# Where the membrane recursion of a spiking delta-rule layer is stepped: eight groups in the front stage, spikes as bytes

## The chip, the cores and the metric

The kernel runs on one core of a Trainium2 chip. The metric is the device time of one execution in microseconds (us), as a median over runs. The engines are TensorE (PE; its weight loads, PEld, overlap the matmuls), VectorE (DVE), ScalarE (ACT), GpSimd (POOL) and SyncE (SP), whose queue issues most transfers. Each engine works through its own list of instructions in order; the lists meet at semaphores. L12 means line 12 of the kernel before.

## The reference, cut to what matters

A two-layer decoder over 64 sequences of 64 positions and 128 features. The change touches one part of layer 1, the delta-rule attention with a spiking neuron: 8 heads of 64 units, so 512 units, each with its own potential `mem` that is stepped along the 64 positions.

```python
q, k, v = heads(h @ Wq), heads(h @ Wk), heads(h @ Wv)   # h: rms norm, causal conv, silu
drive = heads(h @ Wspike, dk)
alpha_base = heads(silu(h @ Wau + bau) @ Wad + bad, dk)
beta_base = h @ Wbeta + bbeta

def step(carry, ins):
    s, mem = carry
    qt, kt, vt, dt, at, bt = ins
    mem = DECAY * mem + dt                      # 0.9
    spike = (mem > THR)                         # 0.5, the forward value
    mem = mem - spike * THR
    alpha = sigmoid(at + asp * spike)           # decay of the state, per unit
    beta = sigmoid(bt + sum(spike * bsp))       # step size, per head
    active = sum(abs(spike)) > 0
    alpha = where(active, alpha, 1); beta = beta * active
    s = s * alpha; pred = kt @ s
    s = s + (beta * kt) (vt - pred)
    return (s, mem), qt @ s
```

The potential depends on `drive` and on nothing of the delta rule, and the delta rule needs the spikes alone.

## The kernel before

The whole decoder is one program of stages one after the other (`run_stage`), each closed by a barrier of all engines. The 4096 tokens stand in NG = 8 groups of T = 512 tokens, that is GB = 8 sequences of S = 64 positions. Features or units lie on the partitions; the 512 units make HDP = 4 blocks of 128, so the drives of one group are 128 partitions x 4 x 512 fp32 values, with position t of every sequence 64 values (256 bytes) apart. Two stages matter.

**Front stage** (`delta_front`, tag "front"). Per group: GpSimd normalises the tokens twice (`zr` for the convolution, L1848, and `zt` for the gate, L1855; group 0's `zr` is VectorE's, L1989); TensorE turns both (L1870, L1876), makes the gate (L1883, L1890) and the drives (L1899, four banks); ScalarE empties the banks (L1959 writes the drives, doubled, so that the threshold is 1); VectorE runs the 4-tap convolution (`conv`, L2006 and L2008). Groups 0 and 1 keep their drives in SBUF, groups 2 to 7 share two buffers and are sent to DRAM (`drive_rows`, L1822 and L1824), 1 MB each. VectorE steps the potential of groups 0 and 1 together: one step is `m = drive[t] - 0.9 * mem` in place (L1997) and `mem = (m > 1) - m` (L1999), both on 128x64 values, each waiting for the one before through a semaphore (`link`). Twenty-four steps are laid between the convolutions of groups 4 to 7, forty behind them. Then two comparisons of 128x2048 make spikes of the potentials (L2023 for group 1, sent to `drive_rows`; L2024 for group 0, put where the next stage reads it).

**Delta stage** (`delta`, tag "delta"). A software pipeline of iterations -2 to 8. In iteration `it` the core is group `it` (chunked delta rule: TensorE's products L2272 and L2285, inverse L2309 and L2331, values and outputs), `front` prepares group `it + 1` (keys, queries, decays, norms), `tail` finishes group `it - 1` (norm, output product, feed-forward), and the order on each engine is written out by hand. The spikes of a group lie in `SPK[g % 2]`. VectorE steps the potential of group `it + 2` (`membrane`, L2820 to L2828, 128x32 values, 127 instructions a group, groups 2 to 7, so iterations 0 to 5) in pieces of 26, 14, 10, 7 and 7 positions between its other work; the first piece stands between `turned(it, 2)` and `masked(it, 5)`, a masked copy (L2778) that TensorE's next products wait for. GpSimd's last work of an iteration is `z_tok` (L2711) and `spikes` (L2687), the comparison of 128x2048 in place. Readers of the spikes are TensorE (`f_cb`, L2205) and VectorE (`f_al`, L2880). SP's queue loads `h`, drives and gates, in one order (`load_h`, `load_drive`, `load_gate`).

## Time and profile before

| | us |
|---|---|
| median of 3 runs | 2706.17 (2694.99 to 2707.96) |
| span of the profiled execution | 2686.7 |
| busy PE / PEld | 2239.4 (83%) / 1568.4 (58%) |
| busy DVE / ACT / POOL | 1613.9 (60%) / 982.9 (37%) / 782.4 (29%) |
| front stage, about | 954 to 1048 |
| delta stage, about | 1049 to 2220 |

The profiled execution's own time is its span of 2686.7 us; the median of the runs lies 19.5 us above it. Busy shares are means over stages with different limits. In a timeline row the first number is the start, the second the time from there to the end of the last of the merged instructions, and brackets give the idle time ahead of it with who ended it. Matmuls are pipelined with modelled ends, so a busy PE need not be PE at its peak.

### The profile page before, as it was taken

How to read it: one execution, taken by the hardware profiler on the slowest of the kernel's cores; microseconds unless marked ns; L12 is line 12 of the kernel's file. 1: busy time of each engine (PE TensorE's matmuls, PEld its weight loads, DVE VectorE, ACT ScalarE, POOL GpSimd, SP SyncE). 2: the span in 40 equal slices, each digit the busy share in tenths (PEclk: the TensorE clock that was granted, in tenths of full speed). 3: DMA queues.
4: the chain of work that ended last, by engine and by line, in shares of the span. 5: the costliest groups of instructions: out<-in, count | busy, mean ns of one | idle time of the engine just before them, and what ended most of it. 6: DMA issues, size and time to landing. Idle time of an engine off the chain costs nothing. (4 is left out here: it accounts for less than half of the span.)

```text
span 2686.7 us, 73844 instructions
## 1 busy us (share of the span) xinstructions
PE 2239.4 (83%) x31032; PEld 1568.4 (58%) x31071; DVE 1613.9 (60%) x4219; ACT 982.9 (37%) x1930; POOL 782.4 (29%) x884
## 2 busy tenths in 40 slices
PE   7898989898877865889999999999999986964675
PEld 4566666666665632465666666666666756653453
DVE  4565555555454366677778787868664713467444
ACT  3444443434322343334343434343434331321222
POOL 0111111111104671325152524343342300111774
PEclk9999998989757977789999999999999975555987
DMA  4000000000021223000000000000000002000114
GB/s 162 9 1 9 9 9 1 5 1 1 1 75 33 62 81 126 6 3 26 3 26 3 26 3 22 7 22 7 3 7 3 7 1 97 2 29 12 52 52 123
DMA packets 42504, 75.78 MB, mean 28 GB/s; under 512 B 5988, under 2 KB 27244, under 8 KB 39620
## 3 DMA queue, kind: packets, MB, share of 16 engines
q1 hardware_dynamic: 35140, 56.63, 6.1%
q0 software_dynamic: 7040, 14.43, 1.9%
q8 instruction: 252, 4.13, 0.6%
q14 instruction: 72, 0.59, 0.1%
HBM read 46.73 MB, written 24.31 MB: 26 GB/s over the span
## 5 line engine op out<-in xcount | busy, mean ns | idle before, releaser
L2778 DVE COPY_PREDICATED delta_neg_a_and_p_t<-delta_level_int,bank 128x256 f32<-128x256 uint8 x384 | 179.3, 536 | 62.5 <-PE bank L2285 62.1
L2309 PEld LDWEIGHTS bank<-delta_inverse,delta_neg_a_and_p_t 64*64 64x64 f32 x5120 | 169.5, 140 | 45.8 <-issue 45.8
L2309 PE MATMUL bank<-delta_inverse,delta_neg_a_and_p_t 64*64 64x64 f32 x5120 | 191.8, 227 | 0.0
L2682 POOL TENSOR_TENSOR delta_scaled_beta_k<-delta_scaled_beta_k,delta_decays 128x256 f32<-128x256 f32 x160 | 124.3, 777 | 221.4 <-issue 162.7
L2512 ACT ACTIVATE delta_two_less_ax<-bank 128x512 f32<-128x512 f32 x160 | 94.9, 597 | 240.4 <-PE bank L2309 238.8
L683 POOL TENSOR_TENSOR attn_probs<-attn_probs,attn_row_sum 128x512 f32<-128x512 f32 x64 | 65.4, 1043 | 385.1 <-DVE attn_row_sum L766 385.1
L2285 PE MATMUL bank<-weights_sb,delta_scaled_beta_k 64*64 64x64 f32 x6144 | 128.0, 228 | 47.9 <-DVE delta_neg_a_and_p_t L2778 43.5
L2285 PEld LDWEIGHTS bank<-weights_sb,delta_scaled_beta_k 64*64 64x64 f32 x6144 | 109.6, 140 | 84.1 <-DVE delta_neg_a_and_p_t L2778 51.1
L303 PE MATMUL bank<-attn_z_self_t,weights_sb 128*128 128x256 f32 x512 | 144.5, 431 | 16.9 <-DVE attn_cross_values L741 12.5
L312 PE MATMUL bank<-attn_w_value_out,attn_z_self_t 128*64 128x512 f32 x512 | 142.5, 682 | 2.0 <-DVE attn_z_value_out L706 1.4
L2331 PE MATMUL bank<-delta_two_less_ax,delta_inverse_t 64*64 64x64 f32 x4096 | 139.0, 223 | 4.1 <-issue 3.9
L2331 PEld LDWEIGHTS bank<-delta_two_less_ax,delta_inverse_t 64*64 64x64 f32 x4096 | 132.5, 140 | 5.6 <-issue 5.3
L750 DVE TENSOR_REDUCE attn_row_max<-bank 128x8 f32<-128x512 f32 x128 | 82.4, 686 | 84.0 <-PE bank L392 54.4
L2518 ACT ACTIVATE delta_inverse<-bank 128x512 f32<-128x512 f32 x128 | 76.4, 598 | 148.8 <-PE bank L2331 148.6
L303 PEld LDWEIGHTS bank<-attn_z_self_t,weights_sb 128*128 128x128 f32 x512 | 102.6, 212 | 44.9 <-issue 22.0
L2185 PE MATMUL bank<-delta_head_rows,norm_sel 16*128 16x512 f32 x192 | 114.5, 699 | 7.8 <-DVE delta_head_rows L2892 3.6
L574 ACT ACTIVATE attn_z_value_out<-bank 128x512 f32<-128x512 f32 x96 | 57.1, 595 | 163.2 <-PE bank L312 163.2
L2700 POOL TENSOR_TENSOR delta_kq_squared<-weights_sb 128x512 f32<-128x512 f32 x64 | 70.8, 1137 | 110.6 <-PE bank L2180 103.8
L1411 POOL DMA_INDIRECT moe_z_sorted<-z_rows,moe_take_row x71 | 68.7, 968 | 106.8 <-DVE moe_take_row L1718 85.5
L2803 DVE TENSOR_TENSOR weights_sb<-weights_sb,delta_decays 128x512 f32<-128x512 f32 x128 | 98.2, 767 | 0.0
L691 POOL TENSOR_TENSOR x_all<-x_all,attn_out_bias 128x256 f32<-128x256 f32 x16 | 11.6, 727 | 278.1 <-DVE attn_z_tokens L786 278.1
L2683 POOL TENSOR_TENSOR delta_decays<-delta_decays 128x256 f32<-128x256 f32 (+4 forms) x160 | 91.7, 573 | 0.0
(545 smaller groups left out, 5139.9 us busy)
## 6 DMA issues: line engine op xcount, KB each, us to landing
delta_drives<-front_drive SPq DMA_DIRECT2D x7, 1024.0 KB, 3.9
weights_sb<-in_w_moe_dram SPq DMA_DIRECT2D x1, 4352.0 KB, 14.8
z_rows<-moe_z_all SPq DMA_DIRECT2D x16, 256.0 KB, 2.3
delta_odd_spikes<-delta_drives SPq DMA_DIRECT2D x4, 1024.0 KB, 5.0
weights_sb<-moe_outs SPq DMA_DIRECT2D x8, 512.0 KB, 7.2
weights_sb<-delta_drives SPq DMA_DIRECT2D x3, 1024.0 KB, 5.0
weights_sb<-in_w_delta_dram SPq DMA_DIRECT2D x1, 2816.0 KB, 9.9
weights_sb<-in_ctx_tok_dram SPq DMA_DIRECT2D x8, 264.0 KB, 5.6
```

Of the source, the lines that this page charges most:

```text
L303: last = pe.matmul(out_[:, i * 256:(i + 1) * 256], wA[:, 0 if kind == "q" else 1, m * 128:(m + 1) * 128], zA[:, g % 2, :], start=True, sto ...
L312: last = pe.matmul(out_[64 * hh:64 * hh + 64, :], zA[:, g % 2, 64 * b:64 * b + 64], vo[:, hh, 512 * half:512 * half + 512], start=True, st ...
L750: dve.tensor_reduce(mx[:, o % 2, h, :], ps[h], AX, ALU.max).then_inc(s["max"], 1)
L2185: return pe.matmul(out_[:, :], nsel[r, j, :], hrows[r, :], start=start, stop=True)
L2285: last = pe.matmul(two[eo][rows(sg), b4 * 64:b4 * 64 + 64], kr[r, hp, t], second(kq[r, g % 2, :, hp, t], c), start=b < 2, stop=True, skip_ ...
L2309: last = pe.matmul(out_[rows(sg), u], AP[rows(sg), hp, eo, b4, 0, :], X[rows(sg), hp, u], start=False, stop=True, skip_group_check=True)
L2331: last = pe.matmul(out_[rows(sg), u], lhsT, rhs, start=b == 0, stop=True, skip_group_check=True)
L2512: act.activation(W[:, hp, :], bank[4 + hp % 2][:, :], ACT.Copy).then_inc(s["w"], 1)
L2682: pool.tensor_tensor(r_[:, :, 0, :], r_[:, :, 0, :], a_[:, :, 1, 0:1].to_broadcast([128, T // (2 * c), c]), ALU.mult)
L2683: pool.tensor_tensor(a_[:, :, 0, 0:1], a_[:, :, 0, 0:1], a_[:, :, 1, 0:1], ALU.mult).then_inc(s["scaled_kr"], 1)
L2778: last = dve.copy_predicated(second(AP[:, hp, eo, :, :, :].rearrange("p b i n -> p (b i) n"), c), m_, PAIR[hp % 2][eo][:, :].rearrange("p ...
L2803: dve.tensor_tensor(v, v, f.unsqueeze(1).to_broadcast([128, 2, m, c]), ALU.mult).then_inc(s["scaled_kq"], 1)
```

## The change

The front stage keeps the drives of all eight groups in SBUF (64 KB per partition), sends none to DRAM, and steps the eight potentials together once the last drive is there: the same 64 positions, each instruction now on 128x256 values, still 64 values apart. None of it lies between the convolutions any more. Then the comparison of group 0 goes to its place in fp32, and those of groups 1 to 7 write bytes (128x2048 uint8) into two buffers, sent to DRAM at 256 KB each; from group 3 on VectorE waits until the buffer's last transfer has landed. GpSimd no longer normalises `zr`: VectorE does it for all groups, two ahead of the convolution, into a part of the weights' region.

In the delta stage the potentials' steps are gone from VectorE. SP loads bytes into one buffer (group g + 1 after GpSimd has widened group g), and GpSimd's comparison becomes a copy from uint8 to fp32 at the same place of its list, for group 1 too, in iteration -1; its wait for the last step becomes waits for the transfer and for the last readers of the buffer that it writes. Two small casts whose results nobody reads (`selb`, `lmi`) leave the end of the attention stage.

```diff
@@ attention stage, end
-                    dve.tensor_copy(selb[:, :, :], self_[:, :, :])
-                    dve.tensor_copy(lmi[:, :, :], lm[:, :, :])
@@ delta_front
-                drive = sb("drive", [128, 4, HDP, T], ctx=ctx)
-                mem = sb("membrane", [128, 2 * HDP * GB], ctx=ctx)
+                drive = sb("drive", [128, NG, HDP, T], ctx=ctx)
+                mem = sb("membrane", [128, NG * HDP * GB], ctx=ctx)
+                spk8 = sb("spike_bytes", [128, 2, HDP, T], U8, ctx=ctx)
...
+                    for g in range(1, NG):
+                        sp.wait_ge(s["spikes"], g + 1)
+                        sp.dma_start(spike_rows[g, :, :, :], spk8[:, g % 2, :, :]).then_inc(spikes_out[g % 2], 16)
...
-                                last = pool.tensor_scalar(zr[:, g % 2, i, :], x_all[:, k, :], mv_all[:, k, 0:1], rms[:, k:k + 1],
...
+                    every = drive[:, :, :, :].rearrange("p g j (b t) -> p (g j b) t", t=S)
 
                     def membrane(t):
-                        m_ = two[:, :, t]
+                        m_ = every[:, :, t]
...
+                    z_rms(0)
+                    z_rms(1)
                     dve.wait_ge(s["pads"], 1)
-                    for g in range(4):
+                    for g in range(NG):
+                        if g + 2 < NG:
+                            z_rms(g + 2)
                         conv(g)
-                    dve.wait_ge(s["drive"], 2 * HDP)
...
+                    dve.wait_ge(s["drive"], NG * HDP)
+                    for t in range(S):
                         membrane(t)
-                    dve.tensor_scalar(drive_of(1), drive_of(1), 1.0, None, ALU.is_gt).then_inc(s["spikes"], 1)
                     dve.tensor_scalar(spk0, drive_of(0), 1.0, None, ALU.is_gt).then_inc(s["spikes"], 1)
+                    for g in range(1, NG):
+                        if g >= 3:
+                            dve.wait_ge(spikes_out[g % 2], 16 * ((g - 1) // 2))
+                        dve.tensor_scalar(spk8[:, g % 2, :, :], drive_of(g), 1.0, None, ALU.is_gt).then_inc(s["spikes"], 1)
@@ delta, SP
-                        sp.dma_start(SPK[g % 2][:, :, :], drive_rows[g, :, :, :]).then_inc(s[f"drive_in{g % 2}"], 16)
+                            sp.wait_ge(s["spikes"], g - 1)
+                        sp.dma_start(spk8[:, :, :], spike_rows[g, :, :, :]).then_inc(s["spikes_in"], 16)
@@ delta, GpSimd
                     def spikes(g):
-                        pool.wait_ge(s["potential"], g - 1)
-                        pool.tensor_scalar(SPK[g % 2][:, :, :], SPK[g % 2][:, :, :], 1.0, None, ALU.is_gt).then_inc(s["spikes"], 1)
+                        pool.wait_ge(s["spikes_in"], 16 * g)
+                        if g >= 2:
+                            pool.wait_ge(s["cb_ps"], nth_of("cb", g - 2))
+                            pool.wait_ge(s["al_rd"], nth_of("al", g - 2, 3))
+                        pool.tensor_copy(SPK[g % 2][:, :, :], spk8[:, :, :]).then_inc(s["spikes"], 1)
@@ delta, VectorE
-                        drive = core and it + 2 < NG
-                        if drive:
-                            membrane(it + 2, 0, 26)
...
-                            membrane(it + 2, 57, S)
```

## Rows read from the trace of the kernel before

**Rows 1.** Busy time by window (PE, PEld, DVE, ACT, POOL; clock), iterations 5 and 6.

```profile
1786.60:1926.30 139.70, 131.16 (x2656) 88.06 (x2655) 108.29 (x264) 58.26 (x100) 52.71 (x59) 0.98 0.02 5
1926.30:2061.60 135.30, 130.33 (x2654) 86.60 (x2654) 75.18 (x138) 57.65 (x99) 47.07 (x58) 0.97 0.02 5
```

**Rows 2.** Timeline of PE: one product of iterations 0, 5 and 6.

```profile
1175.61 0.60 PE L2285 MATMUL bank<-weights_sb,delta_scaled_beta_k 64*64 64x64 f32 x12 [5.00 <-DVE delta_neg_a_and_p_t L2778]
...
1868.31 0.51 PE L2285 MATMUL bank<-weights_sb,delta_scaled_beta_k 64*64 64x64 f32 x18 [3.80 <-DVE delta_neg_a_and_p_t L2778]
...
2004.27 0.52 PE L2285 MATMUL bank<-weights_sb,delta_scaled_beta_k 64*64 64x64 f32 x20 [0.60 <-DVE delta_neg_a_and_p_t L2778]
```

**Rows 3.** Timeline of DVE, iteration 0: last step of the first piece, then masked copy.

```profile
1174.53 0.23 DVE L2828 SCALAR_TENSOR_TENSOR delta_membrane<-weights_sb 128x32 f32<-128x32 f32 x1
1174.79 0.43 DVE L2778 COPY_PREDICATED delta_neg_a_and_p_t<-delta_level_int,bank 128x256 f32<-128x256 uint8 x1
```

**Rows 4.** Groups by line on PE, iteration 5: busy us, mean ns.

```profile
L2161 PE MATMUL bank<-group_conv_out,small_sb 128*64 128x512 f32 x2 | 1.1, 618 | 0.0
```

**Rows 5.** By line: duration min/median/max in ns, first and last start, forms.

```profile
L2826 DVE SCALAR_TENSOR_TENSOR weights_sb<-delta_membrane,weights_sb x186: 204/217/1798, 1158.2 to 1779.9; 128x32 f32<-128x32 f32 x186
L2828 DVE SCALAR_TENSOR_TENSOR delta_membrane<-weights_sb x189: 182/229/1034, 1158.0 to 1780.2; 128x32 f32<-128x32 f32 x189
L1997 DVE SCALAR_TENSOR_TENSOR front_drive<-front_membrane,front_drive x63: 267/278/291, 988.5 to 1042.1; 128x64 f32<-128x64 f32 x63
L1999 DVE SCALAR_TENSOR_TENSOR front_membrane<-front_drive x63: 297/301/436, 988.2 to 1041.8; 128x64 f32<-128x64 f32 x63
```

**Rows 6.** Groups by line and shape on DVE: contiguous values, two lengths.

```profile
L2898 DVE SCALAR_TENSOR_TENSOR delta_scaled_beta_k<-weights_sb,bank 128x512 f32<-128x512 f32 x32 | 21.9, 686 | 47.6 <-PE bank L2185 47.4
L3308 DVE SCALAR_TENSOR_TENSOR gated_weights_t<-bank,gated_decay 128x256 f32<-128x256 f32 x32 | 11.6, 415 | 11.7 <-ACT gated_decay L3218 11.7
```

**Rows 7.** Timeline of DVE: steps at the front stage's end, comparison, next stage.

```profile
1024.75 0.28 DVE L1997 SCALAR_TENSOR_TENSOR front_drive<-front_membrane,front_drive 128x64 f32<-128x64 f32 x1
...
1042.14 0.28 DVE L1997 SCALAR_TENSOR_TENSOR front_drive<-front_membrane,front_drive 128x64 f32<-128x64 f32 x1
1042.45 1.23 DVE L2023 TENSOR_SCALAR front_drive<-front_drive 128x2048 f32<-128x2048 f32 x1
...
1048.82 0.41 DVE L2901 TENSOR_SCALAR delta_half_head_norm<-small_sb 128x4 f32<-128x4 f32 x1 [4.00 <-PEq L118]
```

**Rows 8.** Timeline of ACT: the front stage's last drive.

```profile
1022.85 0.60 ACT L1959 ACTIVATE front_drive<-bank 128x512 f32<-128x512 f32 x1 [0.26 <-PE bank L1899]
```

**Rows 9.** Timeline of PE, front stage: a wait for GpSimd.

```profile
967.70 0.69 PE L1876 MATMUL bank<-const_sb,front_z_tok 128*128 128x128 f32 x2 [1.91 <-POOL front_z_tok L1855]
```

**Rows 10.** The transfers: timeline of SP, by tile (`delta_h`, 256 KB), the page (1 MB).

```profile
1043.71 0.32 SPq L1826 DMA_DIRECT2D delta_drives<-front_drive  x1
...
DMA to landing us min/median/max: 2.0/2.5/3.2
...
delta_drives<-front_drive SPq DMA_DIRECT2D x7, 1024.0 KB, 3.9
```

**Rows 11.** Timeline of DVE: end of the attention stage, start of the next.

```profile
776.37 0.67 DVE L910 CAST sel_bf<-sel_f 8x1024 bf16<-8x1024 f32 x1
776.97 0.24 DVE L911 CAST level_int_sb<-level_sb 128x192 uint8<-128x192 f32 x1
778.31 0.29 DVE L1162 BATCH_NORM_STATS2 moe_bn_stats<-x_all 128x6 f32<-128x128 f32 x1 [1.10 <-PEq L118]
```

**Rows 12.** Timeline of POOL, iterations 5 and 6; a plain copy of the size by line.

```profile
1920.69 5.37 POOL L2687 TENSOR_SCALAR delta_odd_spikes<-delta_odd_spikes 128x2048 f32<-128x2048 f32 x1 [11.93 <-DVE delta_odd_spikes L2824]
1931.64 1.27 POOL L2704 TENSOR_TENSOR delta_two_less_ax<-delta_two_less_ax,delta_o_rstd 128x512 f32<-128x512 f32 x1 [5.57 <-ACT delta_o_rstd L2488]
...
L2671 POOL COPY delta_neg_a_and_p_t<-delta_neg_eye x8: 1890/1926/1927, 1075.4 to 2038.8; 128x2048 f32<-128x2048 f32 x8
```

**Rows 13.** Timeline of PE: first matmul of the delta stage.

```profile
1048.82 1.08 PE L2161 MATMUL bank<-group_conv_out,small_sb 128*64 128x512 f32 x1 [26.00 <-PEq L118]
```

More of the change, by code:

```diff
@@ L1806, in drive_of @@
                 def drive_of(g):
-                    return drive[:, g if g < 2 else 2 + g % 2, :, :]
+                    return drive[:, g, :, :]
                 h_out = [s["h_out0"], s["h_out1"]]
                 gate_out = [s["gate_out0"], s["gate_out1"]]
-                drive_out = [s["drive_out0"], s["drive_out1"]]
+                spikes_out = [s["spikes_out0"], s["spikes_out1"]]
                 @block.sync
@@ L1829, in _ @@
                         sp.wait_ge(gate_out[k], 16 * (NG // 2))
-                        sp.wait_ge(drive_out[k], 16 * (NG // 2 - 1))
-                    sp.wait_ge(s["spikes_out"], 16)
+                        sp.wait_ge(spikes_out[k], 16 * len(range(k or 2, NG, 2)))
                 @block.gpsimd
@@ L1842, in _ @@
                     for g in range(NG):
-                        if g >= 1:
-                            if g >= 2:
-                                pool.wait_ge(s["z_rms_ps"], g - 1)
-                            for i in range(4):
-                                k = 4 * g + i
-                                last = pool.tensor_scalar(zr[:, g % 2, i, :], x_all[:, k, :], mv_all[:, k, 0:1], rms[:, k:k + 1],
-                                                          ALU.subtract, ALU.mult)
-                            last.then_inc(s["z_rms"], 1)
                         if g >= 2:
@@ L1987, in _, with z_rms @@
                     dve.wait_ge(s["rstd"], 1)
-                    for i in range(4):
-                        last = dve.tensor_scalar(zr[:, 0, i, :], x_all[:, i, :], mv_all[:, i, 0:1], rms[:, i:i + 1], ALU.subtract, ALU.mult)
-                    last.then_inc(s["z_rms0"], 1)
-                    two = drive[:, 0:2, :, :].rearrange("p g j (b t) -> p (g j b) t", t=S)
+                    def z_rms(g):
+                        if g >= 2:
+                            dve.wait_ge(s["z_rms_ps"], g - 1)
+                        for i in range(4):
+                            k = 4 * g + i
+                            last = dve.tensor_scalar(zr[:, g % 2, i, :], x_all[:, k, :], mv_all[:, k, 0:1], rms[:, k:k + 1],
+                                                     ALU.subtract, ALU.mult)
+                        last.then_inc(s["z_rms"], 1)
+                    every = drive[:, :, :, :].rearrange("p g j (b t) -> p (g j b) t", t=S)
                     def membrane(t):
-                        m_ = two[:, :, t]
+                        m_ = every[:, :, t]
                         if t >= 1:
@@ L2753, in _ @@
                             z_tok(it)
-                            if it + 2 < NG:
-                                spikes(it + 2)
+                        if 1 <= it + 2 < NG:
+                            spikes(it + 2)
                 @block.vector
@@ L2816, in turned @@
                         dve.transpose(XT[:, hp, :], X[:, hp, :]).then_inc(s["x_t"], 1)
-                    def membrane(g, t0, t1):
-                        dve.wait_ge(s[f"drive_in{g % 2}"], 16 * (g // 2 + g % 2))
-                        rows_ = SPK[g % 2].rearrange("p h (b t) -> p (h b) t", t=S)
-                        for t in range(t0, t1):
-                            m_ = rows_[:, :, t]
-                            if t == S - 1:
-                                dve.scalar_tensor_tensor(m_, mem[:, :], -0.9, m_, ALU.mult, ALU.add).then_inc(s["potential"], 1)
-                            elif t >= 1:
-                                link(dve.scalar_tensor_tensor(m_, mem[:, :], -0.9, m_, ALU.mult, ALU.add))
-                            if t < S - 1:
-                                link(dve.scalar_tensor_tensor(mem[:, :], m_, 1.0, m_, ALU.is_gt, ALU.subtract))
                     def t_gated(g):
@@ L2987, in _ @@
                             f_bk(it + 1)
-                        if drive:
-                            membrane(it + 2, 26, 40)
                         if tail:
@@ L3000, in _ @@
                             f_beta(it + 1)
-                        if drive:
-                            membrane(it + 2, 40, 50)
                         if front:
                             f_kr(it + 1, 0)
-                        if drive:
-                            membrane(it + 2, 50, 57)
                         if tail:
                             t_out(it - 1)
-                        if drive:
-                            membrane(it + 2, 57, S)
                         if front:
@@ L3014, in _ @@
                             f_kr(it + 1, 3)
-            run_stage("delta", "h_in0 h_in1 h_in2 drive_in0 drive_in1 potential spikes gate_in const_set masks au_ps au_rd k_ps k_rd q_ps q_rd al_ps al_rd nrm_part "
+            run_stage("delta", "h_in0 h_in1 h_in2 spikes_in spikes gate_in const_set masks au_ps au_rd k_ps k_rd q_ps q_rd al_ps al_rd nrm_part "
                                "nrm_rd norm root log_root q_sum logit sigmoid beta row_w bias_ps bias bk_ps bk_rd cb_ps cb_rd kr_ps kr_rd ss_ps ss_rd wo_ps wo_rd zz_ps zz_rd f1_ps f1_rd "
```

54 lines of the change are left out of this document (16 added, 38 removed).

## The prediction

> **What bounds the kernel now.** Read first the windows of the delta loop, cut where each group's first products start. Iteration 5 has steps of the potential on VectorE, iteration 6 has none, and the rest of their work is alike: a comparison that the kernel itself makes. Iteration 5 takes 139.7 us with VectorE busy for 108.3 us and TensorE for 131.2 us; iteration 6 takes 135.3 us with VectorE at 75.2 us and TensorE at 130.3 us [rows 1]. So the steps are 33.1 us of VectorE's time per iteration, and 4.4 us of the loop's. TensorE sets the pace; VectorE matters only where TensorE waits for it. Read next TensorE's timeline for its waits. There is one large one per iteration, at the products behind `masked(it, 5)`: 5.00 us in iteration 0, 3.80 us in iteration 5, 0.60 us at the same place of iteration 6 [rows 2]. VectorE's timeline says why: the masked copy follows the last step of the 26-position piece without a gap [rows 3]. The other pieces stand where TensorE has enough to do. Of the 4.4 us, 3.2 us is this wait; 1.1 us is a pair of matmuls (`f_au`) that iteration 6 no longer has [rows 4].
>
> The front stage ends otherwise. Its last drive is written at 1023.45 us [rows 8]; from then VectorE alone steps on until 1042.4 us, then come one comparison, its transfer and the barrier, and the delta stage starts at 1048.8 us [rows 7]. What is put there has no cover at all.
>
> **Delta loop: what goes.** Six iterations lose their steps. The excess of the wait over iteration 6's 0.60 us goes: 4.4 us in iteration 0, and in iterations 1 to 5 3.2 us each (they show the same wait, 3.8 us): 4.4 + 5 x 3.2 = 20.4 us. What is late next is TensorE's own list, as in iteration 6. Bounds: 16 us, if part comes back as other waits; 27 us, 6 x 4.5, if all of the difference between the two windows were due to the steps.
>
> GpSimd's comparison took 5.37 us and stood behind a wait of 11.93 us for the last step [rows 12]. In its place comes a copy from bytes. No row has that form; the nearest are a plain fp32 copy of the size, 1.93 us, and the comparison itself, 5.37 us [rows 12]. It can start when `z_tok` is done, 11.93 us earlier than now, and the next work of GpSimd needs ScalarE's result at 1931.6 us, about 23 us after `z_tok`'s end [rows 12]. So even 5.37 us are covered by TensorE's values and outputs: 0 us. If that cover were gone, 6 x 5.4 = 32 us. GpSimd's new waits are for readers of the iteration before, long done. SP's load of the bytes of group `g + 3` now waits for that copy, and the gate of group `g + 1` is queued behind it; the gate is read an iteration later, so nobody waits. A load of 256 KB for 1 MB costs nothing more.
>
> **Front stage up to the last drive.** VectorE gets 28 more normalisations of 128x128, four a group, and loses the 24 steps (six a group) that stood between the last four convolutions; it is idle for most of each group there, which passes at TensorE's pace, so they cost nothing; a group's four hold a quarter of the values of one comparison of 1.23 us [rows 7], so with their fixed parts about 1.2 us a group, 8 us in all if that cover were gone. GpSimd keeps half of its work; TensorE's early waits for it, such as 1.91 us [rows 9], shrink. I take 2 us off (0 to 4), so the last drive is there at 1021.4 us, not 1023.45 us. The longer idle time of TensorE that follows should cost nothing: already after 26.00 us idle its first matmul pass takes 1.08 us against 0.62 us in the loop [rows 4, 13], so it starts at the lower of its two levels in either kernel.
>
> **The steps at 256 values.** This term decides. At 128x64 the undisturbed pace, from the step at 1024.75 us to that at 1042.14 us, 27 pairs on, is 17.39 / 27 = 0.644 us a pair [rows 7]: 0.278 + 0.301 us busy [rows 5] and 0.065 us between. For the length the same two instructions stand in the trace at 32 values: 0.217 and 0.229 us [rows 5]. So 32 more values cost 0.061 + 0.072 = 0.133 us a pair, 1.9 and 2.25 ns a value. From 64 to 256 values are six such steps: 0.644 + 6 x 0.133 = 1.44 us. Reckoned instead as 0.15 us fixed and the rest per value (2.0 and 2.36 ns) it is 1.48 us. I take 1.45 us; 63 pairs are 91.4 us. The lower bound is the price of contiguous values: (686 - 415) / 256 = 1.06 ns each [rows 6]; 0.644 + 2 x 192 x 0.00106 = 1.05 us, so 66.2 us. The strided pairs are themselves measured at two lengths, so I stay at their end; the upper bound is 1.50 us, 94.5 us.
>
> Against 19.0 us of steps behind the last drive now, 91.4 us is +72.4 us.
>
 The trace agrees, with 1.9 to 2.25 ns a value.
>
> **Comparisons and transfers at the end.** Group 0: 1.15 us (the pitch of the two now). Bytes out: a cast of 192 values to bytes took 0.24 us [rows 11], little over the fixed part, so writing bytes keeps the fast rate, and I take 1.15 us for each of seven too. From group 3 on each waits for the transfer of two before it: 256 KB land 2.5 us after their issue [rows 10], say 2.6 us with the semaphores. The comparisons end at 1.15, 2.3, 4.9, 6.05, 8.65, 9.8 and 12.4 us. Then the last landing, 2.6 us, and 1.2 us to the next stage (now: issued at 1043.7, landed 3.9 us later, next stage at 1048.8 [rows 7, 10]). In all 1.15 + 12.4 + 2.6 + 1.2 = 17.4 us against 6.4 us now: +11.0 us. At one value per cycle (2.3 us each) the chain ends at 17.3 us: 5 us more.
>
> **Attention stage.** The two casts end that stage [rows 11]; without them the barrier comes 0.9 us earlier.
>
> **The sum.** -0.9 - 2.0 + 72.4 + 11.0 - 20.4 = +60.1 us. Span 2686.7 + 60.1 = 2746.8 us. The median of the runs lies 19.5 us above the profiled span; 2706.2 + 60.1 = 2766 us. With the terms at their ends it reaches from 2755 us (27 us gained in the loop, 4 us in the front, pair at 1.42 us) to 2780 us (16 us, 0 us, 1.50 us, slow comparisons).
>
> **The rivals.**
> - One cycle a value. The excess at 64 values could be a fixed latency, so that longer instructions pay 1.06 ns a value. For it: the contiguous rows [rows 6]. Against it: the slope between 32 and 64 values, which holds no fixed part [rows 5]. The steps are 66.2 us, 25 us less: 2741 us.
> - VectorE bounds the loop. If iterations were as long as VectorE's list makes them, each of six would lose its 33.1 us: 198.6 us in place of 20.4 us, so 2588 us, faster than before. For it: VectorE is busy for 78% of iteration 5 and has the largest wait of TensorE. Against it: iteration 6, which is free of the steps, is 4.4 us shorter, not 33. It decides from (60.1 + 20.4) / 6 = 13.4 us an iteration upwards; all of TensorE's idle time in iteration 5 is 8.5 us [rows 1].
> - The widening becomes the wait. If the copy from bytes ran against VectorE so that both stood still, up to 5.4 us in each of seven iterations would show: +38 us, 2804 us. For it: GpSimd's copy moves into a stretch where VectorE works. Against it: the cover of 23 us.
> - The steps stay hidden. Should the scheduler of the front let part of them run before the last drive, there would be less; but the wait for all 32 drives stands in front of the first step, so I give this nothing.
>
> **How the numbers follow.** Forecast 0.82; one cycle a value 0.12; VectorE's loop 0.02; widening 0.04. The range takes in the bounds of the forecast, half of the second case, and some 6 us of spread as in the runs shown: 2742 to 2786 us. A measurement of this kernel can tell about 0.5%, 13.5 us, from no change. Faster: 0.02. Within 0.5%: 0.02, if the first rival meets a larger gain in the loop. Slower: 0.96.
>
> **What would show it.** Right: steps of 128x256 at 0.64 to 0.76 us each and a pair every 1.45 us; a front stage that is some 80 us longer, with TensorE idle for over 100 us at its end; iterations 1 to 5 of 136.5 us, the wait at 0.6 us; bytes compared in 1.2 us, with waits of about 1.4 us for landings; GpSimd's copy under 5.4 us. Wrong: steps at 0.42 to 0.50 us, iterations below 130 us, or a copy that TensorE or VectorE waits for.

## The result and the profile after

The changed kernel takes 2769.4 us (median of 4 runs, 2753.6 to 2777.1) against 2702.4 us (median of 4 runs, 2695.0 to 2708.0) of the kernel before, measured beside it: a ratio of 1.0241, 95% interval 1.0204 to 1.0277 (estimated over the runs, so it isn't the quotient of the two medians). Single executions can take hundreds of microseconds longer with no change of the code (one of `e_pieces` took 3250.8 us, the other five 2676.7 to 2689.8 us); ratios and their intervals leave such executions out, medians don't. The change makes the kernel slower by 2.4%. Its profiled execution has a span of 2751.8 us, 65.1 us more than the one of before; forecast were +60.1 us.

The same boundaries read in both traces tell where the 65.1 us lie:

| stretch | before | after | difference | forecast |
|---|---|---|---|---|
| attention stage, to the first instruction of the next | 778.3 | 785.9 | +7.6 | -0.9 |
| first mixture of experts | 176.3 | 176.2 | -0.1 | 0 |
| front stage, from `front_taps` to the delta stage's first instruction | 94.2 | 172.7 | +78.5 | +81.4 |
| delta stage up to the first products | 49.2 | 49.7 | +0.5 | 0 |
| iterations 0 to 5 of the delta loop | 828.3 | 803.3 | -25.0 | -20.4 |
| iteration 6 to the end | 760.4 | 764.0 | +3.6 | 0 |

First the windows of iterations 5 and 6 of the kernel after, to be held against [rows 1]. The columns are window, length, then busy time with instructions of PE, PEld, DVE, ACT and POOL, granted clock, DMA share, GB/s.

```profile
1850.80:1987.80 137.00, 131.47 (x2653) 87.17 (x2652) 75.23 (x138) 58.23 (x100) 48.88 (x59) 0.98 0.02 5
1987.80:2122.80 135.00, 130.16 (x2654) 87.59 (x2653) 75.00 (x138) 57.67 (x99) 47.08 (x58) 0.97 0.02 5
```

VectorE is busy for 33 us less in iteration 5 than it was, and the iteration is 2.7 us shorter. Its own iteration 6 takes 135.0 us, against 135.3 us before.

The wait that the forecast named, in the timeline of PE at the same product of iteration 4 of after (start, duration, instruction, idle time before it in brackets):

```profile
1793.42 0.39 PE L2272 MATMUL bank<-weights_sb,delta_scaled_beta_k 64*64 64x64 f32 x10 [0.60 <-DVE delta_neg_a_and_p_t L2768]
```

It is 0.60 us, which iteration 6 showed in the kernel before [rows 2].

The front stage's end, in the instructions on `front_drive` of after, grouped by line (duration in ns: minimum, median, maximum; first and last start; form):

```profile
L1986 DVE SCALAR_TENSOR_TENSOR front_membrane<-front_drive x63: 724/727/732, 1024.7 to 1117.9; 128x256 f32<-128x256 f32 x63
L1984 DVE SCALAR_TENSOR_TENSOR front_drive<-front_membrane,front_drive x63: 702/705/711, 1025.5 to 1118.6; 128x256 f32<-128x256 f32 x63
```

And the timeline of DVE of after, from the first step through the comparisons to the delta stage, to be held against [rows 7]:

```profile
1024.73 0.73 DVE L1986 SCALAR_TENSOR_TENSOR front_membrane<-front_drive 128x256 f32<-128x256 f32 x1 [11.73 <-ACT front_drive L1940]
...
1119.38 1.23 DVE L2010 TENSOR_SCALAR weights_sb<-front_drive 128x2048 f32<-128x2048 f32 x1
1120.52 2.36 DVE L2014 TENSOR_SCALAR front_spike_bytes<-front_drive 128x2048 uint8<-128x2048 f32 x2
1123.79 2.36 DVE L2014 TENSOR_SCALAR front_spike_bytes<-front_drive 128x2048 uint8<-128x2048 f32 x2 [0.91 <-DMA delta_spikes<-front_spike_bytes]
1127.05 2.38 DVE L2014 TENSOR_SCALAR front_spike_bytes<-front_drive 128x2048 uint8<-128x2048 f32 x2 [0.90 <-DMA delta_spikes<-front_spike_bytes]
1130.33 1.23 DVE L2014 TENSOR_SCALAR front_spike_bytes<-front_drive 128x2048 uint8<-128x2048 f32 x1 [0.90 <-DMA delta_spikes<-front_spike_bytes]
1134.82 0.41 DVE L2877 TENSOR_SCALAR delta_half_head_norm<-small_sb 128x4 f32<-128x4 f32 x1 [3.26 <-PEq L116]
```

VectorE is idle for 11.73 us until the last drive is written at 1024.70 us, then steps for 94.7 us, with TensorE idle all the while, then compares and sends for 15.4 us. The timeline of PE of after gives that idle time at the next stage's first instruction, where [rows 13] had 26.00 us:

```profile
1134.82 1.94 PE L2150 MATMUL bank<-group_conv_out,small_sb 128*64 128x512 f32 x2 [110.75 <-PEq L116]
```

The widening, in the timeline of POOL, iteration 3 of after (compare [rows 12]):

```profile
1696.80 1.89 POOL L2677 CAST delta_odd_spikes<-delta_spike_bytes 128x2048 f32<-128x2048 uint8 x1
1720.06 1.27 POOL L2694 TENSOR_TENSOR delta_two_less_ax<-delta_two_less_ax,delta_o_rstd 128x512 f32<-128x512 f32 x1 [21.37 <-ACT delta_o_rstd L2475]
```

The copy takes 1.89 us and GpSimd is idle for 21.37 us behind it.

### The profile page after: what moved, and what is told of

It reads as the page before. It is cut to its first block and busy times, and to the rows that moved or that the text cites. A ratio compares the mean times of both kernels' runs of the same rounds, so it can differ in the third digit from the quotient of the medians.

```text
span 2751.8 us, 73107 instructions
## 1 busy us (share of the span) xinstructions
PE 2251.6 (82%) x31071; PEld 1573.6 (57%) x31071; DVE 1480.2 (54%) x3495; ACT 982.6 (36%) x1930; POOL 740.3 (27%) x857
## 5 line engine op out<-in xcount | busy, mean ns | idle before, releaser
L2318 PEld LDWEIGHTS bank<-delta_two_less_ax,delta_inverse_t 64*64 64x64 f32 x4096 | 126.7, 135 | 6.5 <-issue 6.2
L748 DVE TENSOR_REDUCE attn_row_max<-bank 128x8 f32<-128x512 f32 x128 | 82.5, 686 | 87.5 <-PE bank L390 57.9
L2843 DVE TENSOR_TENSOR delta_kq_squared<-delta_silu_or_square,bank 128x512 f32<-128x512 f32 x32 | 21.7, 678 | 158.4 <-PE bank L2231 76.4
L2694 POOL TENSOR_TENSOR delta_two_less_ax<-delta_two_less_ax,delta_o_rstd 128x512 f32<-128x512 f32 x32 | 47.5, 1484 | 220.8 <-ACT delta_o_rstd L2475 220.8
L2150 PE MATMUL bank<-group_conv_out,small_sb 128*64 128x512 f32 x16 | 10.3, 733 | 110.8 <-PEq L116 110.8
```

Source lines behind the costliest of these rows:

```text
L748: dve.tensor_reduce(mx[:, o % 2, h, :], ps[h], AX, ALU.max).then_inc(s["max"], 1)
L2318: last = pe.matmul(out_[rows(sg), u], lhsT, rhs, start=b == 0, stop=True, skip_group_check=True)
```

## The experiments

Two chips were used. On the first (`e_pieces`, `e_no_loop_steps`, `e_position_major`, `e_pieces_front`) the kernel before takes 2706.9 us, on the second (the others) 2753.5 us, so times are compared within a chip alone.

**The wait alone (`e_pieces`).** The theory holds that the steps in the loop cost the one wait behind the 26-position piece, not VectorE's 33 us. This kernel is the one before, with the same 64 steps cut at other positions, so that the first piece is shorter.

```diff
-                            membrane(it + 2, 0, 26)
+                            membrane(it + 2, 0, 18)
...
-                            membrane(it + 2, 26, 40)
+                            membrane(it + 2, 18, 32)
...
-                            membrane(it + 2, 40, 50)
+                            membrane(it + 2, 32, 42)
...
-                            membrane(it + 2, 50, 57)
+                            membrane(it + 2, 42, 57)
```

> The kernel before with its steps kept in the delta loop, but cut elsewhere: the first piece has 18 positions in place of 26, the second and third keep 14 and 10, the fourth has 15 in place of 7, the last keeps 7. The number of instructions is the same. Theory: the steps cost the loop only where the first piece makes TensorE wait for masked(it, 5). The piece ends 8 x 0.51 = 4.1 us earlier, so the wait of 3.8 us goes back to 0.6 us (5.0 in iteration 0), iterations 1 to 5 last 136.5 us and not 139.8 us, and the kernel is about 20 us faster than before (ratio 0.9925). The fourth piece has 5.1 us of idle time behind it, so 4.1 us more fit. Rival: it is VectorE's load as a whole that costs, so the wait turns up at another place and the time stays within 5 us of before.

Measured: 2685.9 us, ratio 0.9931 (0.9908 to 0.9953). Iterations 0 to 5 take 125.4, 136.5, 136.4, 136.3, 136.6 and 136.5 us. Its window of iteration 5, columns as above, and the PE row of the product of iteration 0 that waited 5.00 us in [rows 2]:

```profile
1777.70:1914.20 136.50, 130.02 (x2653) 86.72 (x2652) 108.39 (x264) 58.21 (x100) 52.74 (x59) 0.99 0.02 5
```

```profile
1179.97 0.69 PE L2285 MATMUL bank<-weights_sb,delta_scaled_beta_k 64*64 64x64 f32 x32 [0.96 <-DVE delta_neg_a_and_p_t L2778]
```

VectorE is still busy for 108.4 us and the iteration is as short as that of the changed kernel. So all that the change wins in iterations 1 to 5 was to be had by cutting at another position, at no cost elsewhere.

**No steps in the loop (`e_no_loop_steps`).** The kernel before, leaving out the recursion of groups 2 to 7: only one instruction of the last position stays in each, so the spikes of these groups aren't those of the reference.

```diff
-                        for t in range(t0, t1):
+                        for t in range(S - 1 if t1 == S else t1, t1):
...
-                                dve.scalar_tensor_tensor(m_, mem[:, :], -0.9, m_, ALU.mult, ALU.add).then_inc(s["potential"], 1)
+                                dve.tensor_scalar(m_, m_, 1.0, None, ALU.mult).then_inc(s["potential"], 1)
```

> The kernel before without the potentials' steps of groups 2 to 7 in the delta loop (left out: those 127 instructions a group, one of which is replaced by a product with 1; the spikes of these groups are then comparisons of the drives). GpSimd's comparison of 5.37 us stays. Theory: the loop's gain in the changed kernel (25 us in its trace) comes from the steps' going alone: 20 to 26 us less than before, with iteration 0 about 8 us shorter and 1 to 5 about 3.4 us. Rival: part of it comes from GpSimd, whose copy of 1.89 us stands where the comparison of 5.37 us did and can start earlier: then this kernel gains 3.2 us an iteration and only 4.4 us in iteration 0.

Measured: 2689.4 us, ratio 0.9932 (0.9901 to 0.9962). Without any steps it is no faster than `e_pieces` with all of them. Its iterations take 125.4, 138.5, 139.5, 137.2, 139.8 and 137.0 us, 2 us more on average in 1 to 5 than those of `e_pieces`. Here is a part of its iteration 2 in the timeline of PE, and the window around it:

```profile
1444.89 0.69 PE L2285 MATMUL bank<-weights_sb,delta_scaled_beta_k 64*64 64x64 f32 x32 [0.71 <-DVE delta_neg_a_and_p_t L2778]
...
1452.44 4.87 PE L2185 MATMUL bank<-delta_head_rows,norm_sel 16*128 16x512 f32 x6 [0.76 <-DVE delta_kq_squared L2865]
```

```profile
1446.00:1466.00 20.00, 19.08 (x242) 11.50 (x243) 9.04 (x17) 4.02 (x7) 4.31 (x8) 0.74 0.01 2
```

The wait is gone (0.71 us), but at 1452 us six matmuls of the norms take 4.87 us; the same six take 3.02 us in the changed kernel. The granted clock is 0.74 over these 20 us: TensorE falls to its lower level (1.2 GHz) for a part of them. The same happens at 1729 us. What brings such a fall about isn't settled: it came in iterations 2 and 4 and not in 1, 3 and 5, whose instructions are the same.

The expectation was missed: about 18 us came off by the ratio, not 20 to 26, and 3.9 us in iteration 0 (129.3 us before), not 8. That is what its rival said, which gives the rest to GpSimd's shorter copy. The windows of iteration 0 speak against that rival; they are of before, of after, and of this kernel, columns as above:

```profile
1098.00:1227.30 129.30, 114.80 (x2553) 79.00 (x2552) 99.13 (x243) 46.49 (x80) 44.99 (x54) 0.90 0.04 13
1184.50:1305.90 121.40, 111.60 (x2557) 77.57 (x2556) 66.10 (x117) 46.54 (x80) 40.65 (x54) 0.92 0.03 7
1102.10:1227.50 125.40, 116.48 (x2553) 80.72 (x2552) 66.30 (x118) 46.45 (x80) 44.20 (x54) 0.88 0.04 13
```

TensorE is idle for 14.5 us of the iteration before (its length less the busy time), for 9.8 us in the changed kernel and for 8.9 us here, with GpSimd's comparison still in place. So the waits go with VectorE's steps alone. What this kernel lacks there against the changed one is busy time of TensorE, 116.5 us against 111.6 us for the same matmuls, at a granted clock of 0.88 against 0.92.

**The stride (`e_position_major`).** The changed kernel with the drives stored by position, so that the 256 values of a step stand next to each other. ScalarE's writes, the comparisons and the widening take the stride instead.

```diff
-                drive = sb("drive", [128, NG, HDP, T], ctx=ctx)
+                drive = sb("drive", [128, S, NG, HDP * GB], ctx=ctx)
...
-                            act.activation(drive_of(g)[:, j, :], bank[4 + j][:, :], ACT.Copy, scale=2.0).then_inc(s["drive"], 1)
+                            act.activation(drive[:, :, g, j * GB:(j + 1) * GB].rearrange("p t b -> p b t"),
+                                           bank[4 + j][:, :].rearrange("p (b t) -> p b t", t=S), ACT.Copy, scale=2.0).then_inc(s["drive"], 1)
...
-                        m_ = every[:, :, t]
+                        m_ = every[:, t, :]
```

> The changed kernel with the drives laid out by position: the 256 values of one position stand side by side, ScalarE writes them 1 KB apart, the bytes of a group are stored by position and GpSimd's copy puts them back. Theory: the steps of 0.705 and 0.727 us are slow because each value lies 256 bytes from the next; contiguous they take 0.42 us each, a pair 0.91 us with its gaps, 63 pairs 57 us in place of 94.5 us. The comparison for group 0 gets the stride instead (about 4.5 us, 3.3 us more) and ScalarE's writes stay under TensorE's 0.86 us a bank. In all about 34 us less than the changed kernel, so 2735 us, still slower than before. Rival: the time per value is that of the operation, not of the stride: steps stay above 0.65 us and the kernel within 8 us of the changed one.

Measured: 2733.1 us, ratio 1.0113 (1.0087 to 1.0138), so 1.3% less than the change. Its instructions on `front_drive`, by line:

```profile
L1987 DVE SCALAR_TENSOR_TENSOR front_membrane<-front_drive x63: 425/426/427, 1026.8 to 1083.8; 128x256 f32<-128x256 f32 x63
L1985 DVE SCALAR_TENSOR_TENSOR front_drive<-front_membrane,front_drive x63: 425/426/426, 1027.2 to 1084.3; 128x256 f32<-128x256 f32 x63
L1940 ACT ACTIVATE front_drive<-bank x32: 1032/1076/1120, 980.8 to 1025.7; 128x512 f32<-128x512 f32 x32
```

The same operation on the same number of values takes 426 ns in place of 705 and 727 ns: the stride of 64 values (256 bytes) is what costs, not the length. The steps take 57.9 us (1026.8 to 1084.7), 36.8 us less, and the front stage 138.0 us, 34.7 us less. ScalarE's writes go from 597 to 1076 ns, GpSimd's copies, which put the positions back in order, from 1.89 to 3.92 us, and both hide all the same: the last drive is begun 62.9 us into the stage, against 62.0 us, and iterations 0 to 5 take 807.8 us, against 803.3 us, within what executions of the changed loop differ by (803.3 to 810.9 us). The comparison for group 0 takes 1.90 us, not the 4.5 us expected. `VectorE: DVE Perf Modes` (Trainium skill), section The TRN2 errata, gives (N + 151) / 0.96 ns for an fp32 addition of two tensors and names no stride with it. For N = 256 that is an estimate of 424 ns, with which the contiguous steps agree (425 and 426 ns) and the strided ones of the changed kernel don't (705 and 727 ns).

**The fixed part (`e_halves`).** The changed kernel, its 63 pairs of 256 values taken as two runs of 63 pairs of 128.

```diff
-                    for t in range(S):
-                        membrane(t)
+                    for i in range(2):
+                        for t in range(S):
+                            membrane(t, i)
```

> The changed kernel with the front stage's steps on 128x128 values: first all 64 positions of groups 0 to 3, then all of groups 4 to 7, twice as many instructions. Theory: a strided step costs a fixed part and 2.22 ns a value. From 278 and 301 ns at 64 values and 705 and 727 ns at 256 the line gives 420 and 443 ns at 128, a pair every 0.93 us with its gaps, 126 pairs 117 us, 22.5 us more than in the changed kernel. Rival: the cost per value rises with the length (1.9 ns between 32 and 64 values, 2.22 ns between 64 and 256), so at 128 values the steps lie below the line, at 400 and 425 ns.

**The changed kernel again (`e_changed_again`)**, unaltered, on the same chip:

> The changed kernel once more, unaltered. In its trace the first stage, whose code is that of before but for two casts at its end, is 7.6 us longer than in the trace of before, at a granted clock of 0.86 to 0.94 where that had 0.90 to 0.98. Theory: this belongs to the execution, not to the change: the end of the first stage falls somewhere between 778 and 787 us again, while the front stage (172.7 us) and the loop's iterations repeat within 1 us where their clock is the same. Rival: the changed kernel's first stage is always longer, at 785 us or more.

Measured: 2831.5 us for `e_halves`, 2814.8 us for the changed kernel (one run each), 1.022 times the median of before there. The steps of `e_halves`:

```profile
L1989 DVE SCALAR_TENSOR_TENSOR front_membrane<-front_drive x126: 440/443/446, 1042.2 to 1158.5; 128x128 f32<-128x128 f32 x126
L1987 DVE SCALAR_TENSOR_TENSOR front_drive<-front_membrane,front_drive x126: 417/420/424, 1042.6 to 1159.0; 128x128 f32<-128x128 f32 x126
```

With [rows 5] the step of the potential takes 301, 443 and 727 ns at 64, 128 and 256 values, that of the drive 278, 420 and 705 ns: from 64 to 128 and from 128 to 256 the slope is 2.22 ns a value in each, one line. What the line leaves is about 159 and 136 ns of fixed part. The rival, 400 and 425 ns at 128 values, is out. The front stage takes 195.2 us against 172.9 us in the changed kernel again, +22.3 us where the line gave +22.5 us. The two times differ by 16.7 us only, since the attention stage, with the same code, ended at 785.1 us in one and at 791.4 us in the other.

The expectation for the changed kernel again was met by the front stage (172.9 us) and by iterations 3 to 5, within 1.0 us; iterations 0 to 2 took 1.2 to 4.0 us more, at granted clocks of 0.89 and 0.98 against 0.92 and 0.99. The attention stage ended at 791.4 us, outside the 778 to 787 us expected and where the rival had it, at 785 us or more. All four executions traced on this chip ended it there (785.1, 791.4, 793.6 and 794.8 us); none of them is of the kernel before, so this chip can't tell the change from the chip. This execution has a span 61.2 us longer than the first of the same kernel, and most of that lies in stages that the change leaves alone: the first mixture of experts takes 195.0 us, not 176.2 us, and iteration 6 to the end 793.4 us, not 764.0 us.

**The cover of the widening (`e_widen8`).** The changed kernel; GpSimd makes the same copy eight times per group in place of once.

```diff
+                        for n in range(7):
+                            pool.tensor_copy(SPK[g % 2][:, :, :], spk8[:, :, :]).then_inc(s["widened"], 1)
+                            pool.wait_ge(s["widened"], 7 * (g - 1) + n + 1)
                         pool.tensor_copy(SPK[g % 2][:, :, :], spk8[:, :, :]).then_inc(s["spikes"], 1)
```

> The changed kernel with GpSimd's copy from bytes made eight times in place of once for each group, one after the other (15 us more work? no: 8 x 1.89 = 15.1 us in all, 13.2 us more, plus gaps). Theory: GpSimd is idle for 21.4 us behind the copy, so the loop keeps its length: iterations 1 to 5 at 136 to 137 us, and the copy once costs nothing at all. Rival: the copies run against VectorE's work of the iteration's end and delay the next group's start: iterations 2 us longer or more.

Measured: 2816.8 us, 2.0 us over the changed kernel (one run each). In the timeline of POOL:

```profile
1724.15 13.64 POOL L2678 CAST delta_odd_spikes<-delta_spike_bytes 128x2048 f32<-128x2048 uint8 x7
1737.85 1.89 POOL L2680 CAST delta_odd_spikes<-delta_spike_bytes 128x2048 f32<-128x2048 uint8 x1
1747.40 1.27 POOL L2697 TENSOR_TENSOR delta_two_less_ax<-delta_two_less_ax,delta_o_rstd 128x512 f32<-128x512 f32 x1 [7.66 <-ACT delta_o_rstd L2475]
```

13.6 us more of GpSimd per group, beside VectorE's work, leave 7.66 us of its idle time; iterations 0 to 5 take 805.9 us, against 810.9 us in the changed kernel again; the difference lies in iteration 0 (120.2 and 125.3 us), and iterations 1 to 5 take 137.1 us on average in both. Neither a single copy nor eight of them are waited for.

**The front part alone (`e_pieces_front`).** `e_pieces` with what else the change does ahead of the last drive: no two casts, and all normalisations of `z_rms` on VectorE, two groups ahead, none on GpSimd. The steps of groups 0 and 1 stay where they were, five positions a group in place of six.

```diff
-                            for i in range(4):
-                                k = 4 * g + i
-                                last = pool.tensor_scalar(zr[:, g % 2, i, :], x_all[:, k, :], mv_all[:, k, 0:1], rms[:, k:k + 1],
-                                                          ALU.subtract, ALU.mult)
...
+                    z_rms(0)
+                    z_rms(1)
...
-                        for t in range(6 * (g - 4), 6 * (g - 3)):
+                        if g + 2 < NG:
+                            z_rms(g + 2)
+                        for t in range(5 * (g - 4), 5 * (g - 3)):
```

> As e_pieces, and from the change only its two cheap parts: VectorE normalises for the convolution in the front stage (five steps in place of six between the last convolutions), and the two unread casts are gone. Theory: 20 us as e_pieces, and about 5 us more: the first drives come some 6 us earlier, as in the changed kernel's trace, of which two groups' normalisations of 1.1 us on VectorE's busy stretch take 2 us back, and the casts give 0.8 us. 2677 us, ratio 0.991. Rival: VectorE is the bound of the front stage's second half, so the normalisations cost what they bring, and this kernel is no faster than e_pieces.

Measured: 2677.2 us, ratio 0.9905 (0.9879 to 0.9930). The last drive is begun 63.9 us into the front stage, against 68.2 us in `e_pieces`. Of these 4.3 us, 2.9 us reach the stage's end (91.3 us against 94.3 us), since VectorE still steps behind the last drive. Here are the windows from the stage's start to its last drive, of before, of this kernel, of after and of `e_widen8`, columns as above:

```profile
954.60:1022.85 68.25, 59.27 (x210) 31.07 (x208) 47.46 (x111) 44.27 (x75) 51.37 (x62) 0.83 0.31 125
957.30:1021.25 63.95, 56.88 (x210) 29.95 (x208) 51.31 (x134) 44.19 (x75) 31.20 (x34) 0.86 0.34 134
962.10:1024.10 62.00, 54.93 (x210) 28.85 (x208) 33.48 (x72) 43.90 (x75) 32.32 (x34) 0.89 0.15 56
987.60:1051.50 63.90, 57.38 (x210) 30.49 (x208) 33.46 (x72) 44.23 (x75) 31.46 (x34) 0.86 0.14 54
```

TensorE's idle time, length less busy time, is 9.0 us before and 6.5 to 7.1 us in the three others: 1.9 us less in this kernel and in the changed one. The rest is busy time, for the same 210 matmuls: 59.3 us before, 56.9 us here, 54.9 us in the changed kernel. The second and third ten microseconds of the stage show the clock beside it, first of before, then of this kernel, then of after:

```profile
964.60:974.60 10.00, 7.40 (x25) 4.70 (x25) 3.44 (x5) 4.37 (x7) 10.00 (x13) 0.50 0.07 26
974.60:984.60 10.00, 10.00 (x40) 6.22 (x39) 3.75 (x6) 6.33 (x11) 10.00 (x13) 0.81 0.07 28
...
967.30:977.30 10.00, 10.00 (x40) 6.66 (x39) 6.59 (x15) 6.03 (x11) 9.56 (x11) 0.63 0.08 28
977.30:987.30 10.00, 10.00 (x38) 4.71 (x37) 5.39 (x10) 7.83 (x15) 6.36 (x7) 1.00 0.14 52
...
972.10:982.10 10.00, 10.00 (x43) 6.27 (x42) 7.88 (x16) 7.43 (x13) 10.00 (x12) 0.85 0.15 54
982.10:992.10 10.00, 10.00 (x47) 5.71 (x47) 5.63 (x15) 7.86 (x15) 6.88 (x8) 1.00 0.07 27
```

Before, TensorE, which waits for GpSimd [rows 9], is busy for 7.40 us of the second ten, and the clock is at 0.50; it comes to 0.81 in the third ten. With the normalisations on VectorE, TensorE is full from the second ten on, and the clock there is 0.63 in this kernel and 0.85 in the changed one. From the lower level (0.50) to the higher (1.00), 0.81 is a rise some 24 us into the stage, 0.63 one at 17 us, and 0.85 one at 13 us. All seven traces with these normalisations have 0.60 to 0.85 in the second ten, the three without have 0.50 to 0.54. Among the seven the clock's rise differs between executions: the code of `e_widen8` is that of the changed kernel in this stage, and it has 0.60 there and begins its last drive after 63.9 us, not 62.0.

**Contiguous steps ahead of the end (`e_pieces_early`).** `e_pieces_front`, with the drives of groups 0 and 1 alone stored by position.

```diff
+                early = drive[:, 0:2, :, :].rearrange("p g j t -> p (g j t)").rearrange("p (t g n) -> p t g n", t=S, g=2)
...
+                            if g < 2:
+                                act.activation(early[:, :, g, j * GB:(j + 1) * GB].rearrange("p t b -> p b t"),
+                                               bank[4 + j][:, :].rearrange("p (b t) -> p b t", t=S), ACT.Copy, scale=2.0).then_inc(s["drive"], 1)
...
-                        m_ = two[:, :, t]
+                        m_ = early[:, t, :, :].rearrange("p g n -> p (g n)")
```

> As e_pieces_front, and the drives of groups 0 and 1, which the front stage steps, are laid out by position, so that the steps read and write 64 contiguous values; both comparisons put them back in order. Theory: without the stride a step of 64 values takes (64 + 151) / 0.96 = 224 ns by what the contiguous steps of 256 values showed (426 ns), in place of 278 and 301 ns, a pair 0.51 us in place of 0.644 us: 63 x 0.13 = 8 us less, 1.4 us back for the comparisons (1.9 us each, as in e_position_major). About 7 us less than e_pieces_front: 2670 us, ratio 0.988 to before. Rival: ScalarE's strided writes (1.08 us a bank in place of 0.60 us, for eight banks) delay the groups by as much, and the time is that of e_pieces_front.

Measured: 2719.3 us, ratio 0.9868 (0.9840 to 0.9896), the lowest ratio of all. Its steps, by line, and its timeline of DVE at the stage's end:

```profile
L1998 DVE SCALAR_TENSOR_TENSOR front_membrane<-front_drive x63: 219/226/358, 1019.5 to 1064.5; 128x64 f32<-128x64 f32 x63
L1996 DVE SCALAR_TENSOR_TENSOR front_drive<-front_membrane,front_drive x63: 217/226/359, 1019.7 to 1064.8; 128x64 f32<-128x64 f32 x63
```

```profile
1064.78 0.23 DVE L1996 SCALAR_TENSOR_TENSOR front_drive<-front_membrane,front_drive 128x64 f32<-128x64 f32 x1
1065.04 1.89 DVE L2028 TENSOR_SCALAR front_odd_out<-front_drive 128x2048 f32<-128x2048 f32 x1
1066.85 1.89 DVE L2028 TENSOR_SCALAR weights_sb<-front_drive 128x2048 f32<-128x2048 f32 x1
1072.05 0.41 DVE L2906 TENSOR_SCALAR delta_half_head_norm<-small_sb 128x4 f32<-128x4 f32 x1 [3.31 <-PEq L118]
```

A step takes 226 ns, a pair starts every 0.52 us against 0.644 us [rows 7], and the stage takes 82.5 us against 91.3 us in `e_pieces_front`, 8.8 us less where 7 us were expected. 1.3 us of it were there when the last drive was begun (62.6 us into the stage against 63.9 us), by busy time of TensorE (55.6 us against 56.9 us), at a clock of 0.81 against 0.63 in the second ten microseconds. The two comparisons, which now read with a stride, go from 1.23 to 1.89 us each. The intervals of the two ratios overlap a little and stand for two chips; the stage's length shows the gain better than they do.

## Why the prediction was right, point by point

- **The steps at 256 values: right, the term a little small.** 94.7 us against 91.4 us; a pair every 1.50 us (93.1 us from the first step at 1024.73 us to the one at 1117.9 us, 62 pairs on), which is the upper bound, against 1.45 us. The mis-sized piece is the slope of the drive's step, taken as 1.9 ns a value from its 217 ns at 32 values in the loop. `e_halves` shows 2.22 ns for both steps; the row at 32 values is about 10 ns over that line, and it came from other tiles. The rival of one cycle a value is out. Its slope holds where values are contiguous (1.04 ns a value in `e_position_major` and `e_pieces_early`); its fixed part of 0.644 us a pair doesn't hold there, since the steps take 57.9 us and not its 66.2 us. The estimate of 57 us that the prediction works out from `VectorE: DVE Perf Modes` (Trainium skill), section The TRN2 errata, is right for contiguous steps; "whatever its strides" is the prediction's reading, and the section itself names no stride.
- **Comparisons and transfers: right, the term 2 us large.** 15.4 us against 17.4 us. Bytes are compared in 1.226 us, one every 1.14 us, as taken (1.15 us). The waits are 0.90 us, not 1.4 us, since the 256 KB land in 2.0 us, the lower end of [rows 10], not in 2.5 us. In the case with slow comparisons the prediction's chain ends at 17.0 us by its own steps, not at 17.3 us, which changes nothing that follows.
- **Up to the last drive: right in kind, three times as large.** 6.2 us earlier against 2 us, with a bound of 4 us. The wait itself was sized well: TensorE's idle time shrank by 1.9 us (9.0 to 7.1 us). The step that failed is that only TensorE's waits were counted and its busy time was taken as fixed: it went from 59.3 to 54.9 us for the same matmuls, with the clock's earlier rise. The traces don't ask for a share of the steps that no longer stand between the convolutions: `e_pieces_front`, which has them, and `e_widen8`, which doesn't, begin their last drive at the same 63.9 us, at a clock of 0.63 and 0.60 in the second ten microseconds. The two microseconds from there to 62.0 us differ between executions of the same code. That the fuller TensorE brings the earlier rise is read from ten traces; no run changes it by itself.
- **The delta loop: right.** Iterations 1 to 5 went from 139.8 to 136.4 us on average, 3.4 us against 3.2 us, by the wait, as `e_pieces` shows. Iteration 0 lost 7.9 us against 4.4 us. Of these, 4.7 us are idle time of TensorE (14.5 to 9.8 us), which is the forecast's term; the other 3.2 us are busy time (114.8 to 111.6 us). Five executions have the changed loop, and iteration 0 takes 120.2 to 125.3 us in them, with 111.2 to 115.5 us busy: the changed kernel again took 125.3 us with TensorE idle for 9.8 us, as in its first trace. So these 3.2 us aren't shown to be the change's.
- **The widening: right.** 1.89 us, covered by over 13 us (`e_widen8`).
- **The attention stage: the term right, and lost in something larger.** From the cast at line 907 or 909 to the next stage are 1.52 us in place of 2.28 us, so 0.8 us came off, against 0.9 us. But the stage ended 7.6 us later. With this part of the code alike, it ended at 783.3 and 786.2 us in `e_no_loop_steps` and `e_pieces`, which have the casts, and at 786.5 and 780.6 us in `e_position_major` and `e_pieces_front`, which don't; before had 778.3 us. The two groups lie over each other, so nothing ties the 7.6 us to the change. On the second chip, where the stage ended at 785.1 to 794.8 us without the casts, the kernel before wasn't traced.
- **The sum.** The span grew by 65.1 us against 60.1 us. By the terms that belong to the change it would be 78.5 - 0.8 - 21.8 = about 56 us (21.8 us is -25.0 us less the 3.2 us of iteration 0); the other 9 us lie in the attention stage, in iteration 0's busy time and behind the six iterations, where executions of the same code differ by that much. From iteration 6 to the end, for one, the changed kernel took 3.6 us more than before; `e_no_loop_steps`, whose code there is that of before, took as much more, 764.3 us. The medians, measured side by side, differ by 67.1 us (2769.4 and 2702.4 us); 2766 us started from an earlier median of 2706.2 us. So the nearness of 2766 to 2769 us is in part luck: against the forecast stand -4.2 us up to the last drive, -2.0 us at the transfers and -4.6 us in the loop; and on the other side +3.3 us for the steps, +8.5 us in the attention stage and +4.0 us in the stretches forecast at nothing, which leaves +5.0 us.
- **VectorE bounds the loop: out**, by `e_pieces` and `e_no_loop_steps`.

## What to carry to other kernels

Work that is hidden costs only the wait where it stands in front of something late. Look for that one place, and move the cut there, before moving the work: a shift by 8 positions won in iterations 1 to 5 what the change won there, where the change paid 78.5 us for it in a stage without cover. Where a long chain of small vector steps does lie bare, lay out its operand so that a step's values stand next to each other, and let an engine with idle time write with the stride. And price a longer instruction from rows of the same access pattern at two lengths.

## What the runs showed of the hardware

- A two-tensor operation of VectorE on fp32 with a stride of 256 bytes costs 2.22 ns a value, contiguous (426 - 226) / 192 = 1.04 ns; a comparison with a stride costs 1.89 us for 2048 values a partition in place of 1.23 us; a write of ScalarE of 512 values with a stride of 1 KB 1076 ns in place of 597 ns (in `e_pieces_early`, at 256 bytes, 1083 ns). Other strides weren't run.
- A comparison of 2048 fp32 values that writes bytes takes 1.226 us, as one that writes fp32 does, and GpSimd widens as many bytes to fp32 in 1.89 us, no longer than it copies fp32 [rows 12]; reading the bytes with a stride it takes 3.92 us (`e_position_major`).
- Where TensorE was busy for all of the front stage's second ten microseconds, the granted clock was 0.60 to 0.85 there (seven traces); where it was busy for 7.4 us of them, 0.50 to 0.54 (three traces). The same 210 matmuls of the stage then took 54.9 to 57.4 us of busy time, against 58.3 to 59.3 us. In the delta loop the clock fell for single stretches (0.74 over 20 us) without a difference in the code.
- The same code of the attention stage ended between 778.3 and 786.5 us on the kernels of the first chip and of the first pair of traces; on the second chip it ended between 785.1 and 794.8 us. Differences of one stage below some 8 us aren't read from one pair of traces.
